# Epsilon of the layer norms added on GpSimd, one copy of turned rows moved to VectorE, and a new table of slots

## The chip, the cores and the metric

The kernel runs on one core of a Trainium2 chip. Its time is the device time of one execution in microseconds (us), and the number compared is the median of several executions. Five engines work beside each other, each through its own list of instructions, in order: TensorE (PE: matrix products and transposes), VectorE (DVE), ScalarE (ACT: exponentials and other functions), GpSimd (POOL) and SyncE (SP, which here starts nearly all the DMAs). They wait for one another only through semaphores.

## The reference

The input x holds 8 sequences of 512 tokens with 128 features. A normalised copy of it goes through 6 layers of attention (16 heads of 8 features) and a feed-forward part; the result is added to x, normalised, goes through a gated network, and is added again. All in fp32.

```python
def layer(h, p):
    q = (h @ wq.T + bq_).reshape(bh, sl, H, DH)
    k = (h @ wk.T + bk_).reshape(bh, sl, H, DH)
    scores = jnp.einsum('blhd,bmhd->bhlm', q, k) * inv_sqrt_d
    w_avg = jax.nn.softmax(scores, axis=-1).mean(axis=1)
    new_w = jax.nn.softmax(CSCALE * w_avg + rel[None], axis=-1)
    sa = jnp.einsum('blm,bme->ble', new_w, h)
    h1 = _ln(h + sa, l1w, l1b)      # (x - mean) * rsqrt(var + 1e-5) * w + b
    h2 = _ln(h1, l2w, l2b)
    ff = jax.nn.relu(h2 @ w1.T + b1_) @ w2.T + b2_
    return (_ln(h2 + ff, l3w, l3b), None)

x = x + layers(_layernorm(x))
x = x + gated_network(_layernorm(x))   # silu(x w1) * (x w2), gelu(. h1), gelu(. h2), . w3
```

## The kernel before

One layer of one sequence is a *unit*: 6 layers by 8 sequences make 48 units, numbered t, the layers outside and the sequences inside. A unit has 64 score tiles of 128 rows by 512 columns: 16 groups (4 blocks of tokens by 4 groups of heads) of 4 tiles. Tile s goes through three engines:

- TensorE makes the scores (line 1015, `sc<-kb,qb`) in one of NS = 5 banks of PSUM. It has to wait until ScalarE has read tile s - 5.
- VectorE takes the negated maximum of each row (line 706, `negmax<-sc`).
- ScalarE takes the exponential with that maximum as bias and sums the rows (line 883, `ex<-sc,negmax`). The exponentials stand in a ring of 20 tiles, which TensorE frees by `sum_heads` (line 1033), so exponential s waits for the group of tile s - 20.

The rest of a unit is laid between the tiles. VectorE inverts the sums (712) and GpSimd makes weights from them (525); TensorE averages the heads with them (1033); ScalarE takes exponentials of the mean (889); TensorE turns them (1041), VectorE multiplies by the fixed relative weights (717, `pt<-m,g_sb`), TensorE attends (1022, `m<-hc,pt`), and VectorE adds the residual (724, `res<-hc,m`). Its last column, E, carries the row's sum, by which the rows are still unscaled; so the first norm needs `zz` = EPS/4 * sum * sum in the place of epsilon (791).

A norm is, on VectorE, 4 `bn_stats` (667), then `spread`: 4 `bn_aggr` (658, `mv<-bn`), which give mean and variance, and the addition of epsilon (662, or 664 with `zz`), which gives `veps`. GpSimd then takes veps to the power -0.5 (`power`, 497, `rstd<-veps,nhalf`), subtracts the mean (`center`, 539), multiplies by `rstd` (`scale`, 533), and by the weight and bias rows (543). Norm 0 is the one after attention (`res`), norm 1 the second (`h`), norm 2 the one after the feed-forward part (`xh`), and norm 3 is used for the input at the start and for the 8 outputs of the last layer. After norm 2, TensorE turns the rows into a bank of PSUM (971, called `norm3_turn` in the table), ScalarE copies them out (938, `h3t<-m`, called `norm3_out`), and TensorE multiplies them by the query and key weights of the next layer (`project`, 1022), VectorE taking the queries out (679) and ScalarE the keys (860). This copy exists for the 40 units whose layer is not the last.

What sets the order is a table written out by hand, `STEP`. All engines walk over slots (g, j): g is the unit whose scores are made, j the tile from 0 to 63. A step with the number n is done for unit t in slot 64 t + n, behind the score work of that slot. So n = 95 stands at tile 31 while the next unit's scores are made. `due` (line 124) looks it up. The number only sets where the instruction stands in the list of its engine; when it runs is a matter of the semaphores. Within one slot the order is that of the loop body. The steps `head_...` belong to the gated network at the end, laid between the last unit's steps behind the last score tile.

Of the kernel before, what the change touches and what calls it, by code (L numbers as in the profile page):

```python
# [5 lines left out]
D, B, S, E, H, F = 6, 8, 512, 128, 16, 512  # L6
# [69 lines left out]
    "project": (194, 199),
    "queries": (195,),
    "keys": (197,),
    "split_q": (223, 223, 226, 233),
    "split_k": (207, 207, 218, 230),  # L80
# [4 lines left out]
    "last_spread": (198,),
    "last_power": (202,),
    "last_apply": (203,),
    "last_turn": (205,),
# [1 line left out]
    "first_stats": (0, 0, 0, 2),  # L90
    "first_spread": (8,),
    "first_power": (15,),
    "first_apply": (12, 42),
    "first_turn": (47,),
    "first_out": (46,),
# [68 lines left out]
def build(nc, x, wqk, bqk, w1t, w2t, cols, rows, fw1, fw2, fh1, fh2, fw3, fcols, frow, gmat, sel, ident, out):  # L164
# [3 lines left out]
    with ctx:  # L168
# [188 lines left out]
        def _(sp):  # L357
# [886 lines left out]
```

## Time and profile before

| | us |
|---|---|
| median of 3 runs (2704.07 to 2704.79) | 2704.5 |
| the profiled execution, own time | 2701.24 |
| its span, from first to last instruction | 2699.4 |
| TensorE busy (share of span) | 2533.7 (94%) |
| VectorE busy | 2452.7 (91%) |
| ScalarE busy | 2437.3 (90%) |
| GpSimd busy | 1432.4 (53%) |

The profile is one execution taken by the hardware profiler; its numbers are microseconds unless marked ns. Busy time is the time in which at least one instruction of the engine ran; two neighbours on an engine overlap a little, so the spacing of two starts says more of what an instruction costs than its duration does. A row of a timeline gives the start, the duration, engine and line, the operation with its output and input, and how many equal ones were merged (x7); square brackets tell the idle time before it and who ended it. The mean granted clock of TensorE was 0.994. First and last exponential of a score tile start at 33.3 and 2388.1 us; the stretch from there to the end is the gated network.

### The profile page before, as it was taken

To read this page: it belongs to the slowest core of one execution; us is meant where nothing else is said; L and a number is where in the kernel's file an instruction comes from. 1 tells how busy PE (TensorE), PEld (TensorE's weight loads), DVE (VectorE), ACT (ScalarE), POOL (GpSimd) and SP (SyncE) were. 2 spreads that over 40 slices of the span, in tenths; PEclk is the share of its full clock that TensorE was granted. 3 is DMA by queue.
4 is the path that set the end of the run, shared out by engine and by line. 5 is a ranking of instruction groups with operands and counts; after the bars stand their busy time and mean duration, and the time that the engine had idled before them with its cause. 6 is when DMAs were issued, how large, how long until landed. Compare 5 with 4: busy or idle time off the path is not lost.

```text
span 2699.4 us, 88896 instructions
## 1 busy us (share of the span) xinstructions
PE 2533.7 (94%) x35336; PEld 1213.7 (45%) x35336; DVE 2452.7 (91%) x5616; ACT 2437.3 (90%) x6799; POOL 1432.4 (53%) x1564
## 2 busy tenths in 40 slices
PE   6899999999999999999999999999999999988999
PEld 1344444444444444444444444444444443446777
DVE  6999999999999999999999999999999999963333
ACT  5999999999999999999999999999999999972222
POOL 3567765565555655655656556555566555544000
PEclk8999999999999999999999999999999999999999
DMA  4222212211122112121121122111211211100000
GB/s 130 66 67 72 81 60 65 68 53 56 54 69 64 48 50 68 53 72 54 53 64 46 52 84 69 55 55 53 64 60 53 69 44 55 50 14 17 16 16 24
DMA packets 98913, 152.86 MB, mean 57 GB/s; under 512 B 17857, under 2 KB 81089, under 8 KB 88897
## 3 DMA queue, kind: packets, MB, share of 16 engines
q1 hardware_dynamic: 97936, 146.26, 17.4%
q8 instruction: 278, 4.55, 0.7%
q14 instruction: 139, 1.13, 0.1%
q10 hardware_dynamic: 560, 0.92, 0.1%
HBM read 92.58 MB, written 41.94 MB: 50 GB/s over the span
## 4 chain that ended last, share of the span: by engine, by line
ACT 35%; DVE 35%; PE 19%; issue 9%; POOL 0%; SPq 0%; DMA 0%; POOLq 0%; ACTq 0%; DVEq 0%
ACT ex L883 31%; DVE negmax L706 25%; PE m L1022 4%; PE mean L1110 3%; PE sc L1110 3%; PE mean L1033 3%; DVE pt L717 2%; PE sc L1015 2%; DVE bn L667 2%; ACT ew L889 2%; ACT relu L934 1%; DVE mv L658 1%; DVE veps L662 1%; PE m L1041 1%; PE m L1122 1%
## 5 line engine op out<-in xcount | busy, mean ns | idle before, releaser
L883 ACT ACTIVATE ex<-sc,negmax 128x512 f32<-128x512 f32 x3072 | 2131.2, 824 | 21.7 <-DVE negmax L706 19.9
L706 DVE TENSOR_REDUCE negmax<-sc 128x1 f32<-128x512 f32 x3072 | 1926.2, 676 | 37.3 <-PE sc L1015 22.8
L1015 PE MATMUL sc<-kb,qb 96*32 96x512 bf16 x12288 | 1060.4, 385 | 107.1 <-ACT ex L883 91.1
L883 ACT ACTIVATION_READ_ACCUMULATOR ex<-sc,negmax 128x1 f32 x3072 | 1058.6, 345 | 0.0
L1033 PE MATMUL mean<-ex,rw 128*32 128x512 f32 x6144 | 803.3, 593 | 7.5 <-ACT ew L889 7.5
L1015 PEld LDWEIGHTS sc<-kb,qb 96*32 96x32 bf16 x12288 | 331.6, 94 | 978.8 <-ACT ex L883 826.9
L525 POOL TENSOR_TENSOR rw<-sel_sb,zinv 128x256 f32<-128x256 f32 x384 | 236.0, 615 | 616.8 <-DVE zinv L712 616.7
L1033 PEld LDWEIGHTS mean<-ex,rw 128*32 128x32 f32 x6144 | 199.4, 110 | 157.0 <-issue 80.0
L1022 PE MATMUL m<-hc,pt 128*32 128x129 f32 x6144 | 205.9, 274 | 6.7 <-DVE pt L717 3.5
L1022 PE MATMUL m<-h2t,w_sb 128*32 128x512 f32 x1536 | 204.8, 597 | 5.4 <-ACT relu L934 2.7
L497 POOL TENSOR_TENSOR rstd<-veps,nhalf 128x4 f32<-128x4 f32 x160 | 163.0, 1019 | 78.1 <-DVE veps L664 54.7
L1022 PE MATMUL m<-w_sb,relu 128*32 128x128 f32 x6144 | 200.3, 272 | 0.8 <-ACT relu L934 0.8
L1022 PEld LDWEIGHTS m<-hc,pt 128*32 128x32 f32 x6144 | 170.8, 110 | 48.6 <-DVE pt L717 28.4
L543 POOL TENSOR_TENSOR h<-h,row 128x512 f32<-128x512 f32 x144 | 184.6, 1282 | 7.8 <-POOL h L533 0.4
L1022 PEld LDWEIGHTS m<-w_sb,relu 128*32 128x32 f32 x6144 | 170.5, 109 | 35.8 <-ACT relu L934 23.6
L934 ACT ACTIVATE relu<-m,col 128x512 f32<-128x512 f32 x192 | 163.2, 850 | 12.3 <-PE m L1022 12.3
L539 POOL TENSOR_TENSOR xh<-xh,mv 128x512 f32<-128x512 f32 x48 | 50.1, 1044 | 194.7 <-DVE veps L662 194.7
L889 ACT ACTIVATE ew<-mean 128x512 f32<-128x512 f32 x192 | 133.8, 697 | 0.8 <-PE mean L1033 0.8
L1041 PE MATMUL m<-id_sb,ew 128*128 128x128 f32 x768 | 125.6, 286 | 8.3 <-DVE res L724 0.6
L717 DVE TENSOR_TENSOR pt<-m,g_sb 128x512 f32<-128x512 f32 x192 | 130.1, 678 | 0.0
L1041 PEld LDWEIGHTS m<-id_sb,ew 128*128 128x128 f32 x768 | 80.5, 140 | 75.6 <-issue 39.1
L543 POOL TENSOR_TENSOR h<-h,rb 128x512 f32<-128x512 f32 x48 | 61.6, 1284 | 87.9 <-PE m L971 87.9
(111 smaller groups left out, 2450.1 us busy)
## 6 DMA issues: line engine op xcount, KB each, us to landing
kb<-qk_split SPq DMA_DIRECT2D x288, 128.0 KB
qb<-qk_split SPq DMA_DIRECT2D x568, 64.0 KB
qk_split<-kp SPq DMA_DIRECT2D x144, 128.0 KB, 1.8
qk_split<-qp SPq DMA_DIRECT2D x141, 128.0 KB, 1.8
hc<-hs SPq DMA_DIRECT2D x48, 256.0 KB, 2.7
xin<-x SPq DMA_DIRECT2D x16, 256.0 KB, 2.7
fh_raw<-fh SPq DMA_DIRECT2D x2, 1024.0 KB, 5.2
y_kept<-xin SPq DMA_DIRECT2D x8, 256.0 KB, 2.0
```

The lines of the kernel that those rows point to most:

```text
L497: nc.gpsimd.tensor_tensor(rstd[:, k, :], veps[:, k, :], nhalf[:, :], ALU.pow).then_inc(rstd_ready[k], 1)
L525: nc.gpsimd.tensor_tensor(rw[:, c:c + ZB, :], sel_sb[:, :].rearrange("p (a q) -> p a q", a=1).to_broadcast([P, ZB, QS]), zinv[:, c:c + ZB] ...
L543: nc.gpsimd.tensor_tensor(dst, src[:, :, :], r.to_broadcast([P, NT, E]), op).then_inc(done, 1)
L706: nc.vector.tensor_reduce(negmax[:, s % RT:s % RT + 1], sc[s % NS][:, :], AX, ALU.max, negate=True) \
L717: nc.vector.tensor_tensor(pt[:, i % 2, :, :], m0[:, :].rearrange("p (c l) -> p c l", c=NT), g_sb[:, i, :, :], ALU.mult).then_inc(pt_ready, 1)
L883: nc.scalar.activation(ex[:, s % ET, :], sc[s % NS][:, :], ACT.Exp, bias=negmax[:, c:c + 1], accum_out=zsum[:, c:c + 1]).then_inc(exp_read ...
L889: nc.scalar.activation(ew[:, i % 2, :], mean[:, :], ACT.Exp).then_inc(ew_ready, 1)
L934: nc.scalar.activation(relu[:, c, :], m1[:, :], ACT.Relu, bias=col[RUN[t] % 2][:, C_B1 + c:C_B1 + c + 1]).then_inc(relu_ready, 1)
L1015: ins = nc.tensor.matmul(sc[s % NS][h * QS:h * QS + QS, :], qb[t % 2][:, h % 2, g, h // 2, r:r + QS], kb[t % 2][:, g, h // 2, :], start=Tr ...
L1022: ins = nc.tensor.matmul(dst[n * QS:n * QS + QS], lhsT[:, n * QS:n * QS + QS], rhs, start=start, stop=stop)
L1033: ins = nc.tensor.matmul(mean[n * QS:(n + 1) * QS, :], rw[:, s % RT, :], ex[:, s % ET, :], start=(g == 0), stop=(g == NG - 1))
L1041: ins = nc.tensor.transpose(m0[:, c * P:c * P + P], ew[:, i % 2, c * P:c * P + P], id_sb[:, :])
```

## The change

There are four parts.

1. `spread` on VectorE ends behind the 4 `bn_aggr`. The addition of epsilon, and for norm 0 the two factors of `zz` (before one instruction on VectorE, now two, through a new tile `ze`), stand on GpSimd in `power`, ahead of the power itself: one more small instruction (128 x 4 elements) for norms 1, 2 and 3, and three for norm 0.
2. The subtraction of the mean (`center`) waits for `mv_ready` instead of `veps_ready`. VectorE waits for the earlier `veps` and `zz` before it writes over `mv` and `res`.
3. The copy `h3t<-m` of the 40 units goes from ScalarE to VectorE.
4. Most numbers of `STEP` are new. Two more small memsets stand at the start, and the waits on `filled` count to 7.

```diff
-    "stats0": (66, 76, 77, 83),
-    "spread": (83, 95, 175),
-    "power": (80, 106, 176),
-    "apply0": (82, 85),
+    "stats0": (75, 76, 78, 83),
+    "spread": (83, 94, 175),
+    "power": (84, 110, 178),
+    "apply0": (85, 86),
...
-    "norm3_out": (189,),
+    "norm3_out": (191,),
...
             def power(k, n):
+                if k == 0:
+                    gp.wait_ge(res_ready, n * NT)
+                    nc.gpsimd.tensor_tensor(ze[:, :], res[:, :, E], eps4[:, :], ALU.mult).then_inc(ze_ready, 1)
+                    gp.wait_ge(ze_ready, n)
+                    nc.gpsimd.tensor_tensor(zz[:, :], ze[:, :], res[:, :, E], ALU.mult).then_inc(zz_ready, 1)
+                    gp.wait_ge(zz_ready, n)
+                gp.wait_ge(mv_ready[k], n)
+                nc.gpsimd.tensor_tensor(veps[:, k, :], mv[:, k, :, 1], (eps if k else zz)[:, :], ALU.add).then_inc(veps_ready[k], 1)
                 gp.wait_ge(veps_ready[k], n)
                 nc.gpsimd.tensor_tensor(rstd[:, k, :], veps[:, k, :], nhalf[:, :], ALU.pow).then_inc(rstd_ready[k], 1)
...
             def center(dst, src, k, t):
-                gp.wait_ge(veps_ready[k], t + 1)
+                gp.wait_ge(mv_ready[k], t + 1)
...
-            def spread(k, n, plus):
+            def spread(k, n):
                 dve.wait_ge(bn_ready[k], n * NT)
+                wait_later(dve, veps_ready[k], n - 1)
                 for i in range(NT):
                     ins = nc.vector.bn_aggr(mv[:, k, i, :], bn[:, k, i, :])
                 ins.then_inc(mv_ready[k], 1)
-                dve.wait_ge(mv_ready[k], n)
-                if plus is None:
-                    nc.vector.tensor_scalar(veps[:, k, :], mv[:, k, :, 1], EPS, None, ALU.add).then_inc(veps_ready[k], 1)
-                else:
-                    nc.vector.tensor_tensor(veps[:, k, :], mv[:, k, :, 1], plus, ALU.add).then_inc(veps_ready[k], 1)
...
                 if i == 0:
                     wait_later(dve, centered[0], t)
+                    wait_later(dve, zz_ready, t)
...
                 for t in due("spread", 0, g, j):
-                    nc.vector.scalar_tensor_tensor(zz[:, :], res[:, :, E], EPS / 4, res[:, :, E], ALU.mult, ALU.mult) \
-                        .then_inc(zz_ready, 1)
-                    dve.wait_ge(zz_ready, t + 1)
-                    spread(0, t + 1, zz[:, :])
+                    spread(0, t + 1)
...
+                for t in due("norm3_out", 0, g, j):
+                    dve.wait_ge(xh3t_ready, late_input(t) + 1)
+                    nc.vector.tensor_copy(h3t[:, :], m1[:, :]).then_inc(ht_ready, 1)
...
-                for t in due("norm3_out", 0, g, j):
-                    act.wait_ge(xh3t_ready, late_input(t) + 1)
-                    nc.scalar.activation(h3t[:, :], m1[:, :], ACT.Copy).then_inc(ht_ready, 1)
```

Of the table's other numbers these matter here: the queries' read (`queries`) goes from 195 to 197 and the second product of `project` from 199 to 200; `sum_heads` for group 7 goes from 47 to 50.

First, VectorE in the middle of a unit, from the last statistics of norm 0 (`bn<-res`) to the end of norm 1 (`bn<-h`), before:

```order
L667 BN_STATS bn<-res 128x6
L791 SCALAR_TENSOR_TENSOR zz<-res 128x4
L658 BN_AGGR mv<-bn 128x2 x4
L664 TENSOR_TENSOR veps<-mv,zz 128x4
L706 TENSOR_REDUCE negmax<-sc 128x1 x7
L712 RECIPROCAL zinv<-zsum 128x8
L706 TENSOR_REDUCE negmax<-sc 128x1 x4
L667 BN_STATS bn<-h 128x6 x4
L706 TENSOR_REDUCE negmax<-sc 128x1
L658 BN_AGGR mv<-bn 128x2 x4
L662 TENSOR_SCALAR veps<-mv 128x4
```

and with the change:

```order
L732 SCALAR_TENSOR_TENSOR res<-hc,m 128x129
L674 BN_STATS bn<-res 128x6
L670 BN_AGGR mv<-bn 128x2 x4
L713 TENSOR_REDUCE negmax<-sc 128x1 x10
L719 RECIPROCAL zinv<-zsum 128x8
L713 TENSOR_REDUCE negmax<-sc 128x1
L674 BN_STATS bn<-h 128x6 x4
L670 BN_AGGR mv<-bn 128x2 x4
L713 TENSOR_REDUCE negmax<-sc 128x1 x5
```

The factor `zz` and both additions `veps` are gone; the last residual now stands directly ahead of the last statistics of norm 0, and the statistics of norm 1 directly ahead of their `bn_aggr`, with no score tile between them.

Second, GpSimd at norm 0 in the middle of a unit (`rstd` is the power, `h<-res,mv` subtracts the mean, `h<-h,row` are weight and bias, the casts belong to the splitting of queries and keys), before:

```order
L525 TENSOR_TENSOR rw<-sel_sb,zinv 128x256
L497 TENSOR_TENSOR rstd<-veps,nhalf 128x4
L539 TENSOR_TENSOR h<-res,mv 128x512
L533 TENSOR_TENSOR h<-h,rstd 128x512
L543 TENSOR_TENSOR h<-h,row 128x512
L330 CAST kp<-kf 128x512
L543 TENSOR_TENSOR h<-h,row 128x512
L525 TENSOR_TENSOR rw<-sel_sb,zinv 128x256
L326 CAST qp<-qf 128x512
```

and with the change:

```order
L501 TENSOR_TENSOR ze<-res,eps 128x4
L503 TENSOR_TENSOR zz<-ze,res 128x4
L506 TENSOR_TENSOR veps<-mv,zz 128x4
L508 TENSOR_TENSOR rstd<-veps,nhalf 128x4
L550 TENSOR_TENSOR h<-res,mv 128x512
L327 CAST qp<-qf 128x512
L544 TENSOR_TENSOR h<-h,rstd 128x512
L554 TENSOR_TENSOR h<-h,row 128x512 x2
L536 TENSOR_TENSOR rw<-sel_sb,zinv 128x256
L329 TENSOR_TENSOR kf<-kf,kp 128x512
```

Three small instructions now stand ahead of the power. One cast of 512 columns stands between power and bias before and after, at another place.

Third, the turn of the unit, where the rows for the next layer's projection are copied out (`h3t<-m`). Before it is ScalarE's:

```order
L883 ACTIVATE ex,zsum<-sc,negmax 128x512 x17
L889 ACTIVATE ew<-mean 128x512
L883 ACTIVATE ex,zsum<-sc,negmax 128x512 x14
L938 ACTIVATE h3t<-m 128x512
L883 ACTIVATE ex,zsum<-sc,negmax 128x512 x2
L889 ACTIVATE ew<-mean 128x512
L883 ACTIVATE ex,zsum<-sc,negmax 128x512 x6
L860 ACTIVATE kf<-m,bqk_sb 128x512
```

and with the change it is VectorE's, between the last residual's region and the queries' read (`qf<-m`):

```order
L713 TENSOR_REDUCE negmax<-sc 128x1 x6
L719 RECIPROCAL zinv<-zsum 128x8
L732 SCALAR_TENSOR_TENSOR res<-hc,m 128x129
L713 TENSOR_REDUCE negmax<-sc 128x1 x2
L823 COPY h3t<-m 128x512
L713 TENSOR_REDUCE negmax<-sc 128x1 x3
L719 RECIPROCAL zinv<-zsum 128x8
L713 TENSOR_REDUCE negmax<-sc 128x1 x3
L686 TENSOR_SCALAR qf<-m,bqk_sb 128x512
```

VectorE has one more instruction of 512 columns there, six score tiles ahead of the queries' read.

## Rows read from the trace of the kernel before

**Rows 1.** Busy time by engine in three stretches; x is the number of instructions.

```profile
1000.00:1491.00 491.00, 466.31 (x7124) 212.17 (x7118) 483.37 (x1101) 487.87 (x1391) 283.39 (x311) 1.00 0.19 58
2050.00:2343.00 293.00, 275.75 (x4196) 122.58 (x4192) 289.92 (x699) 292.46 (x834) 163.80 (x174) 1.00 0.18 55
2390.00:2699.00 309.00, 290.50 (x1595) 210.37 (x1594) 119.20 (x237) 91.25 (x123) 39.91 (x35) 0.99 0.05 17
```

**Rows 2.** Groups of instructions by line: VectorE, from 1000 to 1491 us.

```profile
L706 DVE TENSOR_REDUCE negmax<-sc 128x1 f32<-128x512 f32 x641 | 401.8, 675 | 6.2 <-PE sc L1015 2.9
```

**Rows 3.** Groups by line: VectorE, the whole run.

```profile
L730 DVE CAST hid_hi<-fh_raw 128x512 fp32r<-128x512 f32 x32 | 13.9, 435 | 20.8 <-PE mean L1110 20.3
```

**Rows 4.** Timeline of VectorE: start us, duration us, engine, line, operation, count.

```profile
1127.08 0.28 DVE L667 BATCH_NORM_STATS2 bn<-res 128x6 f32<-128x128 f32 x1
1127.28 0.15 DVE L791 SCALAR_TENSOR_TENSOR zz<-res 128x4 f32<-128x4 f32 x1
1127.47 0.38 DVE L658 BATCH_NORM_AGGREGATE mv<-bn 128x2 f32<-128x6 f32 x4
1127.88 0.16 DVE L664 TENSOR_TENSOR veps<-mv,zz 128x4 f32<-128x4 f32 x1
1127.96 4.27 DVE L706 TENSOR_REDUCE negmax<-sc 128x1 f32<-128x512 f32 x7
...
1135.02 0.86 DVE L667 BATCH_NORM_STATS2 bn<-h 128x6 f32<-128x128 f32 x4
...
1136.58 0.37 DVE L658 BATCH_NORM_AGGREGATE mv<-bn 128x2 f32<-128x6 f32 x4
1136.98 0.57 DVE L662 TENSOR_SCALAR veps<-mv 128x4 f32<-128x4 f32 x1
1137.46 2.47 DVE L706 TENSOR_REDUCE negmax<-sc 128x1 f32<-128x512 f32 x4
1139.86 0.67 DVE L717 TENSOR_TENSOR pt<-m,g_sb 128x512 f32<-128x512 f32 x1
1140.46 1.27 DVE L706 TENSOR_REDUCE negmax<-sc 128x1 f32<-128x512 f32 x2
...
1149.40 0.37 DVE L658 BATCH_NORM_AGGREGATE mv<-bn 128x2 f32<-128x6 f32 x4
1149.80 0.17 DVE L662 TENSOR_SCALAR veps<-mv 128x4 f32<-128x4 f32 x1
1149.87 3.07 DVE L706 TENSOR_REDUCE negmax<-sc 128x1 f32<-128x512 f32 x5
```

**Rows 5.** Timeline of ScalarE, from 1110 to 1113 us.

```profile
1110.84 0.66 ACT L938 ACTIVATE h3t<-m 128x512 f32<-128x512 f32 x1
1111.32 0.76 ACT L883 ACTIVATE ex<-sc,negmax 128x512 f32<-128x512 f32 x1
...
1111.98 0.77 ACT L883 ACTIVATE ex<-sc,negmax 128x512 f32<-128x512 f32 x1
```

**Rows 6.** Timeline of ScalarE, from 1018 to 1020 us.

```profile
1018.88 0.82 ACT L860 ACTIVATE kf<-m,bqk_sb 128x512 f32<-128x512 f32 x1
1019.45 0.83 ACT L883 ACTIVATE ex<-sc,negmax 128x512 f32<-128x512 f32 x1
```

**Rows 7.** Timeline of GpSimd, from 1110 to 1160 us.

```profile
1128.13 1.02 POOL L497 TENSOR_TENSOR rstd<-veps,nhalf 128x4 f32<-128x4 f32 x1 [1.11 <-DVE veps L664]
1129.12 1.04 POOL L539 TENSOR_TENSOR h<-res,mv 128x512 f32<-128x512 f32 x1
...
1133.21 1.28 POOL L543 TENSOR_TENSOR h<-h,row 128x512 f32<-128x512 f32 x1
...
1136.92 0.61 POOL L330 CAST qp<-qf 128x512 bf16<-128x512 f32 x1
```

**Rows 8.** Groups by line: GpSimd, the whole run.

```profile
L581 POOL TENSOR_TENSOR rb<-row 128x128 f32<-128x128 f32 x6 | 2.7, 455 | 0.0
```

**Rows 9.** Groups by line: ScalarE, the whole run.

```profile
L905 ACT ACT_TABLE_LOAD x6 | 7.7, 1283 | 0.1
```

More of the change, by code:

```diff
@@ L45 @@
 STEP = {
-    "invert_sums": (12, 18, 26, 37, 42, 52, 58, 66),
-    "row_weights": (14, 16, 28, 42, 45, 50, 67, 73),
-    "sum_heads": (21, 22, 25, 26, 32, 34, 45, 47, 52, 57, 61, 64, 69, 72, 73, 75),
+    "invert_sums": (12, 17, 29, 36, 42, 51, 61, 66),
+    "row_weights": (9, 19, 29, 44, 44, 51, 67, 69),
+    "sum_heads": (21, 21, 25, 27, 32, 34, 45, 50, 52, 56, 61, 64, 69, 71, 74, 75),
     "exp_mean": (25, 47, 63, 73),
     "transpose_mean": (30, 53, 68, 79),
-    "relative": (35, 56, 73, 78),
@@ L52 @@
-    "attend": (40, 59, 76, 82),
-    "residual": (40, 61, 76, 82),
-    "stats0": (66, 76, 77, 83),
-    "spread": (83, 95, 175),
-    "power": (80, 106, 176),
-    "apply0": (82, 85),
-    "norm1_weight": (90,),
-    "norm1_bias": (91,),
+    "relative": (35, 55, 74, 78),
+    "attend": (40, 59, 76, 81),
+    "residual": (40, 61, 76, 83),
+    "stats0": (75, 76, 78, 83),
+    "spread": (83, 94, 175),
+    "power": (84, 110, 178),
+    "apply0": (85, 86),
+    "norm1_weight": (88,),
+    "norm1_bias": (88,),
@@ L60 @@
     "stats1": (94, 94, 94, 94),
-    "apply1": (107, 107),
+    "apply1": (107, 110),
     "norm2_turn": (143,),
     "norm2_out": (142,),
-    "token_weight": (141,),
+    "token_weight": (136,),
     "token_bias": (143,),
     "up": (146, 151, 156, 158),
-    "relu": (146, 150, 153, 158),
+    "relu": (146, 150, 153, 157),
     "down": (163, 165, 170, 172),
     "add": (172,),
-    "stats2": (173, 174, 174, 174),
-    "apply2": (175, 176),
+    "stats2": (173, 173, 174, 174),
+    "apply2": (175, 178),
@@ L72 @@
     "norm3_turn": (191,),
-    "norm3_out": (189,),
-    "norm3_weight": (178,),
+    "norm3_out": (191,),
+    "norm3_weight": (180,),
     "norm3_bias": (182,),
[L76 to L80, printed above, removed]
+    "project": (195, 200),
+    "queries": (197,),
+    "keys": (200,),
+    "split_q": (213, 223, 233, 233),
+    "split_k": (211, 222, 222, 229),
     "last_weight": (185,),
-    "last_bias": (192,),
@@ L83 @@
-    "last_add": (193,),
+    "last_bias": (194,),
+    "last_add": (194,),
     "last_stats": (193,),
[L85 to L88, printed above, removed]
+    "last_spread": (195,),
+    "last_power": (198,),
+    "last_apply": (198,),
+    "last_turn": (203,),
     "last_keep": (203,),
[L90 to L95, printed above, removed]
@@ L108 @@
-    "head_gelu": (69, 82, 85, 87, 92, 94, 99, 110, 111, 117, 118, 134, 153, 156, 170, 173),
-    "head_split": (94, 100, 114, 115, 118, 145, 145, 148),
+    "first_stats": (0, 0, 0, 1),
+    "first_spread": (6,),
+    "first_power": (6,),
+    "first_apply": (12, 14),
+    "first_turn": (48,),
+    "first_out": (45,),
+    "first_token": (44,),
+    "first_project": (50, 55),
+    "first_queries": (52,),
+    "first_keys": (55,),
+    "first_split_q": (55, 61, 61, 61),
+    "first_split_k": (55, 62, 64, 68),
@@ new lines @@
+    "head_high": (0, 3, 18, 25, 30, 32, 38, 53),
+    "head_low": (9, 17, 31, 39, 47, 64, 64, 67),
+    "head_first": (66, 66, 70, 70, 73, 76, 78, 79),
+    "head_silu": (64, 65, 65, 67, 67, 73, 84, 92),
+    "head_gate": (63, 69, 71, 71, 74, 76, 78, 85),
+    "head_square": (75, 83, 87, 93, 94, 97, 110, 112, 112, 125, 127, 135, 141, 157, 179, 192),
+    "head_gelu": (79, 88, 92, 93, 97, 103, 110, 120, 120, 122, 135, 135, 161, 169, 172, 177),
+    "head_split": (88, 93, 98, 110, 128, 132, 144, 169),
@@ L200, in build @@
         rstd = sb("rstd", [P, 4, NT])
-        nhalf = sb("nhalf", [P, NT])
+        nhalf, eps, eps4 = sb("nhalf", [P, NT]), sb("eps", [P, NT]), sb("eps4", [P, NT])
+        ze = sb("ze", [P, NT])
         h1 = sb("h1", [P, NT, E])
@@ L283, in build @@
         sa_ready = sem("sa_ready")
-        zz_ready = sem("zz_ready")
+        ze_ready, zz_ready = sem("ze_ready"), sem("zz_ready")
         res_ready = sem("res_ready")
@@ L423, in _ @@
                 sp.dma_start(qk_dram[0, 3 + n, :, :], kp[n][:, :]).then_inc(kept, 16)
-            sp.wait_ge(filled, 5)
+            sp.wait_ge(filled, 7)
             sp.wait_ge(q_kept, 48)
@@ L686, in _ @@
                 wait_later(dve, first_ready, b)
-                spread(3, b + 1, None)
+                spread(3, b + 1)
                 dve.wait_ge(rstd_ready[3], b + 1)
@@ L800, in _ @@
                     wait_later(dve, centered[1], t)
-                    spread(1, t + 1, None)
+                    spread(1, t + 1)
                 for t in due("add", 0, g, j):
@@ L824, in _ @@
                     wait_later(dve, centered[3], b - PRE)
-                    spread(3, b + 1, None)
+                    spread(3, b + 1)
                 for b in due("first_queries", 0, g, j):
@@ L834, in _ @@
                 for t in due("last_spread", 0, g, j):
-                    spread(3, B + OUTER[t] + 1, None)
+                    spread(3, B + OUTER[t] + 1)
                 for n in range(2 * CH):
@@ L871, in _ @@
             first_copy(1)
-            act.wait_ge(filled, 5)
+            act.wait_ge(filled, 7)
             act.wait_ge(q_kept, 48)
```

19 lines of the change are left out of this document (5 added, 14 removed).

## The prediction

> **What bounds the kernel now.** I read the busy shares first: TensorE, VectorE and ScalarE all stand at 90% or more, GpSimd at 53%, so the end is set by three engines that pass tiles round, and the table of stretches has to say which. From 1000 to 1491 us VectorE is busy 483.37 of 491.00 us and ScalarE 487.87 [rows 1]; 641 score maxima fall into it [rows 2], which is 10.0 units of 64, so a unit takes 49.1 us. VectorE has 7.6 us idle in ten units, 0.76 per unit. ScalarE's busy time overstates its load: two exponentials in a row start 0.66 us apart (1111.32 and 1111.98) although each is shown with over 0.7 us [rows 5]. Counted by starts ScalarE needs 64 x 0.66 + 5 x 0.48 (four exponentials of the mean and the copy, the copy being 1110.84 to 1111.32 [rows 5]) + 6 x 0.57 (h2t, four relu and the keys; the keys' row is 1018.88 to 1019.45 [rows 6]; that the others are like it is my reading of their kind and size) = 42.2 + 2.4 + 3.4 = 48.1 us, 1.0 below the period. VectorE by its idle time needs 49.1 - 0.76 = 48.3. So VectorE is the fullest engine, ScalarE 0.2 behind it, and 0.7 us per unit is lost because only five banks lie between them: where one has a bunch of extra work, the other runs dry. In the last layer (2050 to 2343) VectorE's idle time is 3.1 us in 293, and TensorE alone carries the stretch behind the last exponential, 290.5 of 309 us [rows 1].
>
> **Part 1, epsilon on GpSimd.** Timeline of VectorE, one unit [rows 4].
> Norm 0: from the last statistics (1127.08) to the next maximum (1127.96) 0.88 us. What stays is statistics of 0.28, a hand-over of 0.03 (the `bn_aggr` that end at 1127.85 are followed by the dependent addition at 1127.88), and the four `bn_aggr`, 0.37, of which the last 0.08 overlap with an independent follower, as the four maxima's 2.47 end 0.07 behind the next start (1137.46, 1139.86). That is 0.28 + 0.03 + 0.29 = 0.60. The last residual now stands right ahead of these statistics and has to finish first; that costs about the same 0.07 + 0.03 = 0.10. Saved: 0.18.
> Norm 1: from `bn_aggr` (1136.58) to the next maximum (1137.46) 0.88, now 0.29; but the statistics stand right ahead now, which costs 0.11. Saved: 0.48.
> Norm 2: 1149.40 to 1149.87, 0.47, now 0.29. Saved: 0.18.
> Together 0.84 us per unit. Norm 1's addition is the dearest: it is shown with 0.57 us against 0.17 for the same instruction in norm 2. It ended at 1137.55, within 0.02 of the GpSimd cast that began at 1136.92 with 0.61 [rows 7]: it stood waiting for that cast. The Trainium skill (SBUF — State Buffer, "Who interferes with whom") says that a VectorE instruction in a 2-port mode, which an SBUF-to-SBUF tensor_scalar can be, is locked out for the whole of a GpSimd instruction that began first; by that rule the trace agrees (0.57 against 0.17). The skill (Perfetto Trace Analysis, "Optimizing Scalar/DVE Operations") also warns that moving work from VectorE to GpSimd may not help because they share that port. That would cost something only where VectorE keeps instructions that use the shared port; the two kinds that the trace shows doing so go away, so I price it at nothing.
> Norms of units 0 to 46 end under score tiles: 47 x 0.84 = 39.5 us. The extra spreads of norm 3 save 0.18 each: 7 outputs and 6 inputs, 2.3 us.
>
> On GpSimd the new instructions are not in the trace. The nearest rows: 128 columns with 0.455 us [rows 8] and 512 columns with 1.28 [rows 7], which put 4 columns at 0.455 - 124 x 0.825/384 = 0.19 us; and from above the power itself on the same 4 columns, 1.02 us [rows 7]. I take 0.19 plus 0.08 between dependent ones, since a power is another computation than a sum. Five of them are 1.4 us per unit on an engine with 20 us free (283.39 busy of 491 [rows 1]). What counts is norm 0's chain. Before, the power began at 1128.13, the bias ended at 1133.21 + 1.28 = 1134.49 [rows 7], and VectorE came for it at 1135.02 [rows 4]: 0.53 us to spare. Counted from the last statistics' start, `mv` is now ready after 0.28 + 0.03 + 0.37 = 0.68 instead of 0.77 us; `ze` and `zz` run beside it; the addition and the power follow, so the power starts after about 0.68 + 0.05 + 0.27 = 1.00 us, against 1128.13 - 1127.08 = 1.05 before. VectorE itself comes 0.28 earlier. So 0.3 us stay to spare and nothing is paid.
>
> **Part 2, the copy on VectorE.** 40 copies of 512 fp32 columns out of PSUM. The trace has none on VectorE. Nearest from PSUM: the product `pt`, 1139.86 to 1140.46, 0.60 us [rows 4]; the maxima are as long. From below, a cast of 512 columns within SBUF, 0.435 us shown [rows 3], some 0.36 by starts. I take 0.60, the row with the same source. The Trainium skill (VectorE: DVE Perf Modes, "Why PSUM operands drop a tier") says that an fp32 operand in PSUM leaves only the 1x mode; by it the upper row holds, by the SBUF cast the copies would be 9.6 us cheaper in all. No run here shows yet which. 40 x 0.60 = 24.0 us more on VectorE. ScalarE is relieved of 40 x 0.48 = 19.2 us, which buys nothing directly, since it isn't the fullest. The copy waits for the turn in the same slot; TensorE issues that behind the score tile whose maximum VectorE takes first (0.60), longer than the four transposes, so I price this wait at nothing. Behind it on VectorE are queued the next maxima; if the turn is late, they are.
>
> **Part 3, the slots.** VectorE now needs 48.3 - 0.84 + 0.60 = 48.1 us per inner unit, ScalarE 47.6. Whether the 0.76 us of idle time shrinks hangs on the bunches. Two of VectorE's are thinner (the statistics of norms 0 and 1 with their additions), and at the unit's turn the loads of both come nearer to each other. Against it, `sum_heads` of group 7 goes from slot 47 to 50, two slots behind the exponential that needs its place, and the second projection is now three slots behind the queries' read instead of four. I take 0.1 us less idle per unit, 40 x 0.1 = 4 us; the ends are 0.76 less and 0.45 more.
> At the start GpSimd's addition stands ahead of two powers on the way to the first tile: +0.3 us. In the tail ScalarE switches its function tables once more than before, 1.28 us [rows 9]; TensorE's list is the same but for two or three exchanged places: I count +1.3.
>
> **Sum.** -39.5 - 2.3 + 24.0 - 4.0 + 0.3 + 1.3 = -20.2 us on the profiled execution, 2701.24 to 2681.0. The median of the runs shown is 3.3 above that execution; so the forecast is 2704.5 - 20 = 2684 us (-0.75%).
>
> **Rivals.**
> A, the waits go too. VectorE waits for TensorE at the turn of the unit (2.9 us of its idle time there is behind score tiles [rows 2]); if the copy falls into such gaps and the thinner bunches halve the idle time, 40 x 0.38 = 15 us go instead of 4: 2673 us. For it speaks that ScalarE's load drops by 0.5 us per unit as well; against it, that VectorE remains the fullest.
> B, the slots eat it. A late turn, the queries' read that TensorE's second projection waits for, or group 7's `sum_heads` costs 0.45 us more idle time per unit, 18 us over 40 units, where I counted 4 less: 2684 + 22 = 2706, and half of it 2695. For it: TensorE is busy 466 of 491 us [rows 1] and packed at the unit's turn.
> C, slower, by one mechanism: a small GpSimd instruction costs like the power, 1.0 us, not 0.19. `ze`, `zz` and the addition then end 3 x 1.08 = 3.2 us behind the last residual instead of 1.0, the power starts 2.2 us late, and with 0.3 us to spare VectorE stands still 1.9 us ahead of norm 1's statistics in each of 47 units: +89 us, 2704.5 - 20 + 89 = 2773. It decides from about 0.35 us each, where 3 x (0.35 + 0.08) is the 1.3 us that the spare time allows. For it speaks only that the power's row has the same shape; against it the line through 128 and 512 columns.
> That the change doesn't do what it says (VectorE's list as long as before) is excluded by the order of its instructions.
>
> **How the numbers follow.** Forecast 0.62 (its own range 2677 to 2692), A 0.15, B 0.15, C 0.08. A change of under 0.2%, 5.4 us, is what a measurement of this kernel can't tell from none. Below 2699.1 lie the forecast, A, and a third of B: 0.82. Within 0.2% half of B and a little of C's mild forms: 0.09. Slower: the rest of B and of C: 0.09. The range goes from 2669 (A) to 2702 (B in part).
>
> **What would show it.** Right: no `zz` and `veps` on VectorE, a copy with starts 0.60 apart, a unit of 48.5 to 48.7 us, VectorE's idle time 0.6 to 0.7 per unit; small GpSimd additions of about 0.2 us; no idle time ahead of `bn<-h`; the stretch behind the last exponential within 2 us of 311. Wrong: additions near 1 us and VectorE waiting ahead of `bn<-h` (C); a period of 49 us with waits for the turn, or exponentials waiting for `sum_heads` (B); a period under 48.4 (A). If ScalarE turned out as the fullest, 0.48 and not VectorE's 0.24 us would be what a unit gains, and the first step would be wrong.

## The result

| | before | with the change |
|---|---|---|
| median, us | 2704.35 | 2676.53 (2675.93 to 2677.58) |
| ratio | | 0.9898 (0.9885 to 0.9910) |
| span of the profiled execution, us | 2699.4 | 2674.7 |
| first exponential of a score tile starts at | 33.3 | 33.5 |
| last one starts at | 2388.1 | 2364.5 |
| from there to the end of the span | 311.3 | 310.2 |

The change is 1.0% faster, 28 us by the medians; 20 were forecast. The two profiled executions lie 24.7 us apart, because the one before ran 3 us below its median. Nearly all of that lies under the score tiles: the stretch from the first to the last exponential is 23.8 us shorter, the start 0.2 longer, the tail 1.1 shorter. By the starts of the exponentials, a unit of the four middle layers takes 48.45 us instead of 49.11 (21.3 us in 32 units); the first and the last layer give 1.3 and 1.2 us, each over its 8 units.

The same three stretches of the changed kernel (the stretch and its length, then PE, PEld, DVE, ACT and POOL busy, granted clock, DMA share, GB/s); they answer to [rows 1], and the first two windows again hold ten and six units:

```profile
1000.00:1485.00 485.00, 465.32 (x7148) 204.90 (x7140) 478.32 (x1072) 484.17 (x1382) 293.72 (x362) 1.00 0.20 59
2030.00:2322.00 292.00, 273.94 (x4198) 119.83 (x4191) 286.94 (x674) 291.54 (x835) 176.01 (x213) 1.00 0.18 55
2368.00:2674.00 306.00, 288.77 (x1594) 209.40 (x1592) 119.14 (x239) 92.66 (x124) 41.67 (x43) 0.99 0.05 17
```

VectorE is idle for 6.7 us in ten units, where it was 7.6. The norms of one unit on VectorE, which answer to [rows 4]:

```profile
1116.60 0.34 DVE L732 SCALAR_TENSOR_TENSOR res<-hc,m 128x129 f32<-128x129 f32 x1
1116.98 0.29 DVE L674 BATCH_NORM_STATS2 bn<-res 128x6 f32<-128x128 f32 x1
1117.31 0.38 DVE L670 BATCH_NORM_AGGREGATE mv<-bn 128x2 f32<-128x6 f32 x4
1117.60 5.44 DVE L713 TENSOR_REDUCE negmax<-sc 128x1 f32<-128x512 f32 x9
...
1124.60 0.86 DVE L674 BATCH_NORM_STATS2 bn<-h 128x6 f32<-128x128 f32 x4
1125.55 0.38 DVE L670 BATCH_NORM_AGGREGATE mv<-bn 128x2 f32<-128x6 f32 x4
1125.85 2.45 DVE L713 TENSOR_REDUCE negmax<-sc 128x1 f32<-128x512 f32 x4
...
1138.64 0.37 DVE L670 BATCH_NORM_AGGREGATE mv<-bn 128x2 f32<-128x6 f32 x4
1138.92 2.45 DVE L713 TENSOR_REDUCE negmax<-sc 128x1 f32<-128x512 f32 x4
...
1149.46 0.68 DVE L823 COPY h3t<-m 128x512 f32<-128x512 f32 x1
1150.06 1.88 DVE L713 TENSOR_REDUCE negmax<-sc 128x1 f32<-128x512 f32 x3
```

`zz` and `veps` are gone. From the last statistics of norm 0 (1116.98) to the next maximum 0.62 us; `bn_aggr` to maximum 0.30 and 0.28 in norms 1 and 2; the copy out of PSUM takes 0.60 by starts. So the forecast's upper row was the right one. The wait of norm 1's addition behind a GpSimd cast [rows 4, 7] has no place any more. On GpSimd, norm 0 now reads (answers to [rows 7]):

```profile
1117.03 0.20 POOL L501 TENSOR_TENSOR ze<-res,eps 128x4 f32<-128x4 f32 x1 [0.37 <-DVE res L732]
1117.30 0.21 POOL L503 TENSOR_TENSOR zz<-ze,res 128x4 f32<-128x4 f32 x1
1117.83 0.20 POOL L506 TENSOR_TENSOR veps<-mv,zz 128x4 f32<-128x4 f32 x1 [0.32 <-DVE mv L670]
1118.11 1.02 POOL L508 TENSOR_TENSOR rstd<-veps,nhalf 128x4 f32<-128x4 f32 x1
...
1121.84 2.63 POOL L554 TENSOR_TENSOR h<-h,row 128x512 f32<-128x512 f32 x2
```

and the new addition over the whole run:

```profile
L506 POOL TENSOR_TENSOR veps<-mv,eps 128x4 f32<-128x4 f32 x112 | 23.0, 205 | 24.7 <-DVE mv L670 24.6
```

A small addition takes 0.2 us, the power behind it 1.02 as before. The two instructions merged in the last row of the timeline are norm 0's weight and bias; they end at 1124.47, and VectorE comes for them at 1124.60 without waiting (it starts 0.08 us before the shown end of its previous instruction).

### The profile page after: what moved, and what is told of

It is laid out like the page before. It is cut to its first block and busy times, and to the rows that moved or that the text cites. A ratio compares the mean times of both kernels' runs of the same rounds, so it can differ in the third digit from the quotient of the medians.

```text
span 2674.7 us, 89003 instructions
## 1 busy us (share of the span) xinstructions
PE 2523.1 (94%) x35336; PEld 1185.6 (44%) x35336; DVE 2423.9 (91%) x5448; ACT 2421.3 (91%) x6760; POOL 1486.5 (56%) x1822
## 5 line engine op out<-in xcount | busy, mean ns | idle before, releaser
L891 ACT ACTIVATE ex<-sc,negmax 128x512 f32<-128x512 f32 x3072 | 2096.2, 767 | 14.9 <-DVE negmax L713 10.5
L1020 PE MATMUL sc<-kb,qb 96*32 96x512 bf16 x12288 | 1048.6, 385 | 92.4 <-ACT ex L891 72.3
L891 ACT ACTIVATION_READ_ACCUMULATOR ex<-sc,negmax 128x1 f32 x3072 | 883.8, 288 | 0.0
L1038 PE MATMUL mean<-ex,rw 128*32 128x512 f32 x6144 | 790.0, 594 | 7.6 <-ACT ew L897 7.6
L1020 PEld LDWEIGHTS sc<-kb,qb 96*32 96x32 bf16 x12288 | 321.4, 94 | 996.7 <-ACT ex L891 862.6
L1038 PEld LDWEIGHTS mean<-ex,rw 128*32 128x32 f32 x6144 | 189.1, 110 | 147.4 <-issue 69.8
L942 ACT ACTIVATE relu<-m,col 128x512 f32<-128x512 f32 x192 | 144.5, 753 | 10.3 <-PE m L1027 10.3
L897 ACT ACTIVATE ew<-mean 128x512 f32<-128x512 f32 x192 | 124.5, 648 | 0.0
L544 POOL TENSOR_TENSOR h<-h,rstd 128x512 f32<-128x512 f32 x96 | 99.7, 1039 | 7.5
```

The costliest lines, as they stand in the source:

```text
L891: nc.scalar.activation(ex[:, s % ET, :], sc[s % NS][:, :], ACT.Exp, bias=negmax[:, c:c + 1], accum_out=zsum[:, c:c + 1]).then_inc(exp_read ...
L897: nc.scalar.activation(ew[:, i % 2, :], mean[:, :], ACT.Exp).then_inc(ew_ready, 1)
L942: nc.scalar.activation(relu[:, c, :], m1[:, :], ACT.Relu, bias=col[RUN[t] % 2][:, C_B1 + c:C_B1 + c + 1]).then_inc(relu_ready, 1)
L1020: ins = nc.tensor.matmul(sc[s % NS][h * QS:h * QS + QS, :], qb[t % 2][:, h % 2, g, h // 2, r:r + QS], kb[t % 2][:, g, h // 2, :], start=Tr ...
L1038: ins = nc.tensor.matmul(mean[n * QS:(n + 1) * QS, :], rw[:, s % RT, :], ex[:, s % ET, :], start=(g == 0), stop=(g == NG - 1))
```

## Where the limit stands

Two neighbouring tiles of ScalarE show what sets the unit. Before, at the end of VectorE's stretch (norm 2 at slots 44 to 47):

```profile
1148.40 0.70 ACT L883 ACTIVATE ex<-sc,negmax 128x512 f32<-128x512 f32 x1
...
1149.51 0.69 ACT L883 ACTIVATE ex<-sc,negmax 128x512 f32<-128x512 f32 x1 [0.31 <-DVE negmax L706]
```

With the change, at the same place:

```profile
1137.88 0.70 ACT L891 ACTIVATE ex<-sc,negmax 128x512 f32<-128x512 f32 x1
...
1138.76 0.69 ACT L891 ACTIVATE ex<-sc,negmax 128x512 f32<-128x512 f32 x1
```

Two starts that follow each other without a wait are 0.66 us apart. Here they are 1.11 and 0.88 apart: 0.45 us of waiting before, 0.21 after. The bracket tells only what lies beyond the shown end of the last instruction (0.31), and after the change there is none at all, though ScalarE waited. So I went through ScalarE's starts over ten units of each kernel, took 0.66 us off each exponential, 0.48 off the mean's exponentials and the copy, and 0.57 off the others, and what was over 0.03 us I counted as waiting, by the tile behind which it stands ("46: 0.45" is 0.45 us per unit between the exponentials of tiles 46 and 47). The rest of the period is ScalarE's own load.

| kernel | unit, us | load of ScalarE | waits of ScalarE | at tiles |
|---|---|---|---|---|
| before | 49.12 | 48.2 | 0.88 | 19: 0.13, 43: 0.30, 46: 0.45 |
| the change | 48.46 | 47.75 | 0.71 | 5: 0.14, 19: 0.19, 43: 0.16, 46: 0.21 |
| e1 | 50.17 | 48.3 | 1.92 | 3: 0.86, 9: 0.13, 19: 0.44, 43: 0.16, 46: 0.22, 55: 0.08 |
| e2 | 48.88 | 48.2 | 0.67 | 25: 0.07, 43: 0.39, 46: 0.21 |
| e3 | 49.15 | 47.8 | 1.37 | 3: 0.60, 43: 0.28, 46: 0.43 |
| e4 | 48.74 | 47.8 | 0.94 | 3: 0.44, 43: 0.29, 46: 0.21 |
| e5 | 49.83 | 48.2 | 1.59 | 3: 0.93, 9: 0.13, 19: 0.15, 43: 0.16, 46: 0.22 |
| e6 | 49.02 | 47.8 | 1.25 | 5: 0.26, 19: 0.50, 43: 0.16, 46: 0.22, 55: 0.08 |
| e7 | 49.04 | 47.8 | 1.27 | 5: 0.26, 19: 0.18, 43: 0.16, 46: 0.22, 63: 0.39 |
| e8 | 48.98 | 48.3 | 0.66 | 5: 0.14, 19: 0.11, 43: 0.19, 46: 0.21 |
| e9 | 48.93 | 48.3 | 0.64 | 19: 0.23, 43: 0.20, 46: 0.21 |
| e10 | 48.46 | 47.8 | 0.64 | 5: 0.12, 19: 0.17, 43: 0.15, 46: 0.21 |
| e11 | 49.05 | 47.8 | 1.26 | 5: 0.12, 19: 0.16, 43: 0.15, 44: 0.18, 45: 0.32, 46: 0.32 |
| e12 | 48.97 | 48.3 | 0.64 | 19: 0.24, 43: 0.20, 46: 0.21 |

In the kernel before and in the change ScalarE waits at three or four places and runs without a gap everywhere else. The change takes 0.49 us off its load (the copy) and 0.17 off its waits.

For whom it waits isn't the same at each place. Behind tiles 19 and 46, and with the copy on VectorE behind 3, 5 and 63, the next exponential starts 0.03 us after the end of its maximum: it waited for VectorE. Behind tile 43 it did not. There the maximum had been ready for 0.75 to 1 us in every kernel of the table but e11 (0.39), and the exponential starts 0.14 us after the end of TensorE's `sum_heads`, which frees its place in the ring. Before:

```profile
1145.89 1.03 PE L1033 MATMUL mean<-ex,rw 128*32 128x512 f32 x8
1146.11 0.99 ACT L883 ACTIVATE ex<-sc,negmax 128x512 f32<-128x512 f32 x1
1147.07 0.70 ACT L883 ACTIVATE ex<-sc,negmax 128x512 f32<-128x512 f32 x1
```

So 0.15 to 0.39 us per unit of waiting is TensorE's, not VectorE's; no run moved that step by itself. The wait behind tile 3 in e1 and e5 is of this kind too.

## The experiments

Three parts (epsilon on GpSimd, the copy on VectorE, the table) make eight combinations. Medians in us, each less the median of the kernel before in the same session (2702.8 to 2705.0); the 95% intervals of the ratios reach 0.0009 to 0.0014 to either side, 2.5 to 4 us.

| | copy on ScalarE | copy on VectorE |
|---|---|---|
| old table, epsilon on VectorE | 0 | +1.8 (e3) |
| old table, epsilon on GpSimd | -12.3 (e2) | -18.3 (e4) |
| new table, epsilon on VectorE | +42.2 (e1) | +0.7 (e6) |
| new table, epsilon on GpSimd | +24.3 (e5); copy at slot 189: -11.4 (e9) | -27.8 (the change) |

The texts put on record ahead of the runs speak of theories. Theory 1 is the prediction's: the fullest engine, VectorE, sets the unit. Theory 2 is its rival, given anew for each run. Theory 3 is that a step came too late in its list. Theory 4 is that the limit goes from engine to engine within a unit, and only the load of the one whose stretch it is counts.

**e1**, the kernel before with the whole new table.

```diff
-    "spread": (83, 95, 175),
-    "power": (80, 106, 176),
+    "spread": (83, 94, 175),
+    "power": (84, 110, 178),
...
-    "norm3_out": (189,),
+    "norm3_out": (191,),
...
-    "queries": (195,),
+    "queries": (197,),
```

> The kernel before with the new table of slots and nothing else: epsilon stays on VectorE, the copy h3t stays on ScalarE. Theory 1 (the fullest engine sets the unit, the table moves only the waits a little, as predicted): 4 us less than before, 2700 us, period of a unit 49.0 us. Theory 2 (most of the 28 us come from the table, which evens out bunches and removes waits that hide inside the spacing of the score maxima): at least 15 us less, 2689 us or below, period 48.7.

2746.9 us, ratio 1.0155 (1.0141 to 1.0169). Both theories missed: the table alone makes the kernel slower. From 1000 to 1490 us TensorE waits 10 times, 13.3 us in all, for the copy `h3t`. e5 has the same fault, and e9 its cause.

**e2**, epsilon on GpSimd as in the change (parts 1 and 2 of it, which no run took apart), the old table, the copy on ScalarE. Against the change, beside the table:

```diff
-                for t in due("norm3_out", 0, g, j):
-                    dve.wait_ge(xh3t_ready, late_input(t) + 1)
-                    nc.vector.tensor_copy(h3t[:, :], m1[:, :]).then_inc(ht_ready, 1)
+                for t in due("norm3_out", 0, g, j):
+                    act.wait_ge(xh3t_ready, late_input(t) + 1)
+                    nc.scalar.activation(h3t[:, :], m1[:, :], ACT.Copy).then_inc(ht_ready, 1)
```

> Epsilon's additions on GpSimd, the old table, the copy h3t still on ScalarE. Theory 1: VectorE's load falls by 0.84 us per unit to 47.5, ScalarE with 48.1 becomes the fullest, so a unit falls by 0.5 to 0.7 us and the kernel by 25 to 33 us, 2672 to 2680 us. Theory 2: the waits of the old table stay, 8 to 12 us less, about 2694 us.

2692.4 us, 0.9955 (0.9942 to 0.9967): -12.3, near theory 2's number. VectorE's instructions other than the maxima take 0.96 us less per unit, counted from start to start in the trace, where 0.84 was forecast. The unit is only 0.24 shorter: the other 0.73 turn up behind VectorE's score maxima as waiting, most of it too short to be shown as idle time (9.2 us in 485, before 7.6).

**e3**, the copy on VectorE at slot 191, the rest as before.

```diff
-    "norm3_out": (189,),
+    "norm3_out": (191,),
...
+                    nc.vector.tensor_copy(h3t[:, :], m1[:, :]).then_inc(ht_ready, 1)
...
-                    nc.scalar.activation(h3t[:, :], m1[:, :], ACT.Copy).then_inc(ht_ready, 1)
```

> The copy h3t on VectorE (its slot 191, where the turn stands, else the old table), epsilon still on VectorE. Theory 1: VectorE is the fullest and gets 0.60 us more in 40 units, +24 us, 2728 us. Theory 2: VectorE waits at this place anyway and ScalarE is relieved; +5 to +10 us at most, 2712 us.

2706.5 us, 1.0008 (0.9999 to 1.0017). Not +24: ScalarE's load falls by 0.4 to 0.5 us per unit, and its waits rise by 0.49, with a new one of 0.60 behind tile 3.

**e4**, the change with the old table (the copy at 191).

```diff
-    "power": (84, 110, 178),
+    "power": (80, 106, 176),
...
-    "queries": (197,),
+    "queries": (195,),
```

> Epsilon on GpSimd and the copy on VectorE, with the old table (only the copy's slot is 191). It is the change without its slots. Theory 1: -40 + 24 = -16 us, 2688 us. Theory 2: the loads alone bring little, -5 us, 2699 us. The difference to the change's 2676.5 is what the table is worth once the loads are moved.

2686.4 us, 0.9932 (0.9919 to 0.9946): -18.3. Theory 1's number, but not for its reason, since its two terms (-40 and +24) are wrong by themselves. ScalarE in this kernel, at tile 3, behind the copy and the queries' read on VectorE (slots 191 and 195):

```profile
1010.90 0.82 ACT L891 ACTIVATE ex<-sc,negmax 128x512 f32<-128x512 f32 x1
...
1012.01 0.69 ACT L891 ACTIVATE ex<-sc,negmax 128x512 f32<-128x512 f32 x1 [0.19 <-DVE negmax L713]
```

1.11 us instead of 0.66. In the change, with the queries' read at 197, there is no wait at tile 3 and 0.14 at tile 5. The table is worth 9.5 us (e4 to the change), and this is where the unit shows most of it: waits at tile 3 or 5 from 0.44 to 0.14, at 43 from 0.29 to 0.16, at 19 from nothing to 0.19. That it is the queries' number which did it is read from the place of the wait; it wasn't moved by itself.

**e5**, the change with the copy on ScalarE, at the table's slot 191 (diff as in e2).

> The change with the copy h3t left on ScalarE (its slot 191): what the move of the copy is worth inside the change. Theory 1 (VectorE is the fullest): VectorE gets 24 us lighter, ScalarE at 48.1 per unit becomes the limit; 2666 to 2672 us, 5 to 10 us faster than the change. Theory 2 (with epsilon gone VectorE and ScalarE are level, and a unit is limited by ScalarE's load plus its waits): 5 to 15 us slower than the change, 2682 to 2692 us.

2727.1 us, 1.0089 (1.0076 to 1.0103): 52 above the change, far beyond both. TensorE's waits from 1000 to 1485 us (us in total, times, the longest):

```profile
PE m L1027 <- ACT h3t L943: 13.3, 10, 1.3
```

Ten times 1.3 us, once per unit, the query projection at slot 195 waits for the copy. `sum_heads` stands behind it in TensorE's list and is late by it, and ScalarE in turn waits for that, 0.93 us per unit behind tile 3. Of this the profile shows what lies beyond the shown ends:

```profile
ACT ex L888 <- PE mean L1038: 6.7, 10, 0.7
```

**e9**, e5 with one number back.

```diff
-    "norm3_out": (191,),
+    "norm3_out": (189,),
```

> The kernel of run e5 (change with the copy h3t left on ScalarE) with the copy at slot 189 instead of 191. In e5 TensorE's query projection waited 1.3 us for this copy in every unit. Theory 3 (lateness: at 191 ScalarE's list, which runs some four tiles behind TensorE's, reaches the copy after TensorE wants it at 195): the wait goes and the kernel falls by 40 us or more, to 2680 to 2688 us, 3 to 11 us above the change, which is then what moving the copy off ScalarE is worth. Rival (ScalarE's load is the cause): it stays above 2715 us.

2693.5 us, 0.9960 (0.9947 to 0.9972). The 36 us were the lateness. The lists run apart: when TensorE starts this projection in e9, it has begun the scores of tile 3 and ScalarE is at the exponential of tile 63 of the unit before, four tiles behind. So slot 191 (tile 63) on ScalarE comes no earlier than slot 195 (tile 3) on TensorE. It stays 16.4 above the change, more than the 3 to 11 expected: that is the worth of the copy's move with the new table, 0.41 us in each of 40 units, close to the 0.48 that ScalarE is relieved of. ScalarE is then shown busy for the whole stretch (its waits are hidden by the shown durations) and VectorE is idle for 13.3 us in ten units:

```profile
1000.00:1485.00 485.00, 461.75 (x7080) 208.76 (x7084) 471.73 (x1048) 484.39 (x1380) 291.06 (x360) 1.00 0.20 59
```

**e6**, the new table and the copy on VectorE, epsilon on VectorE as before: e1 with the copy moved.

```diff
+                    nc.vector.tensor_copy(h3t[:, :], m1[:, :]).then_inc(ht_ready, 1)
...
-                    nc.scalar.activation(h3t[:, :], m1[:, :], ACT.Copy).then_inc(ht_ready, 1)
```

> The new table and the copy on VectorE, epsilon still on VectorE. Theory 1: +24 - 4, 2724 us, VectorE's idle time per unit under 0.7. Theory 2: the table makes up for the copy, 2700 to 2710 us. Against the change's 2676.5 it gives what epsilon on GpSimd is worth with everything else in place: 0.84 x 47 = 40 us by the prediction.

2703.4 us, 1.0001 (0.9992 to 1.0010). Against it the change is 28.5 us faster: epsilon's worth with everything else in place, where VectorE is loaded with the copy. With the copy on ScalarE and the old table it was 12.3. ScalarE's load is the same in e6 and the change; the waits differ, behind tile 19, where norm 0's `spread` stands, 0.50 against 0.19 us, and behind 5, 0.26 against 0.14.

**e7**, the change with a second copy on VectorE.

```diff
+                    wait_later(dve, spared, t)
+                    nc.vector.tensor_copy(spare[:, :], m1[:, :]).then_inc(spared, 1)
                     nc.vector.tensor_copy(h3t[:, :], m1[:, :]).then_inc(ht_ready, 1)
```

> The change with one more VectorE copy of the same 512 columns out of the same bank in each of 40 units, into a spare bf16 tile, 0.60 us by starts. It measures how much of VectorE's load reaches the unit. Theory 1: VectorE is the fullest, all of it, +24 us, 2700 us. Rival: VectorE has 0.7 us of idle time per unit that takes it in, under +8 us.

2698.6 us, 0.9985 (0.9976 to 0.9993): 22 to 24 above the change. The second copy stands ahead of the needed one, which it delays too: TensorE now waits 0.4 us for that one in each unit, and 0.05 us of it reach ScalarE, behind tile 3. The rest is VectorE's load itself: ScalarE gets a new wait of 0.39 us behind tile 63, for the maximum, and 0.12 more behind 5. At this place VectorE's load counts in full.

**e8**, the change with a second read of the keys' bank on ScalarE.

```diff
+                    act.wait_ge(k_ready, late_input(t) + 1)
+                    wait_later(act, spared, t)
+                    nc.scalar.activation(spare[:, :], m1[:, :], ACT.Identity,
+                                         bias=bqk_sb[LAYER_OF[late_input(t)] % 2][:, 1:2]).then_inc(spared, 1)
                     keys(late_input(t))
```

> The change with one more ScalarE activation of 512 columns out of the keys' bank in each of 40 units, into a spare bf16 tile, 0.57 us by starts. Theory 1: ScalarE has about 0.8 us to spare in a unit of 48.4 (its load is 47.6), so under +8 us, 2684 us at most. Rival: the change left ScalarE as the limit with its waits, +23 us, 2699 us.

2696.8 us, 0.9979 (0.9970 to 0.9987): 20 to 22 above the change for 23 us of work. Its waits stay as they were (0.66 against 0.71 us per unit), so the work goes on top. Theory 1 fell here: ScalarE had nothing to spare.

**e10, e11 and e12**, the change with one more instruction of 512 columns at another slot in 40 units, on VectorE at 24 (e10, shown) and 40 (e11), on ScalarE at 52 (e12).

```diff
+    "extra": (24,),
...
+                for t in due("extra", 0, g, j):
+                    wait_later(dve, spared, t)
+                    nc.vector.tensor_reduce(spare[:, :], g_sb[:, 0, :, :].rearrange("p c l -> p (c l)"), AX, ALU.max, negate=True) \
+                        .then_inc(spared, 1)
```

and for e12, in ScalarE's list:

```diff
+                for t in due("extra", 0, g, j):
+                    wait_later(act, spared, t)
+                    nc.scalar.activation(spare[:, :], g_sb[:, 0, :, :].rearrange("p c l -> p (c l)"), ACT.Copy).then_inc(spared, 1)
```

> The change with one more VectorE maximum of 512 columns (0.60 us, from SBUF into a spare column) at slot 24 in 40 units, where ScalarE has its relus and VectorE shows its waits for score tiles. Theory 4 (the limit goes from engine to engine within a unit, and only the one whose stretch it is counts): VectorE is not it here, at most +8 us, 2677 to 2685 us. Rival (VectorE as full as e7 said, anywhere in the unit): +20 to +24 us, 2697 to 2700.

> The same instruction at slot 40, in VectorE's own stretch (residual, the feed-forward addition and norm 2 lie at 40 to 47). Theory 4: nearly all of 0.60 x 40 us, +18 to +24 us, 2695 to 2700 us. Rival (the load counts as a sum over the unit): the same as at slot 24, within 3 us.

> The change with one more ScalarE copy of 512 columns (from SBUF into a spare bf16 tile, about 0.5 us) at slot 52 in 40 units, where ScalarE has nothing but exponentials from 48 to 62. Theory 4: ScalarE is not the limit here, at most +8 us, 2677 to 2685 us. Rival (ScalarE's load counts wherever it stands, as at the keys in e8): +17 to +20 us, 2694 to 2697.

e10: 2679.1 us, 0.9907 (0.9893 to 0.9920), 2 above the change, which lies within the intervals. e11: 2700.0 us, 0.9981 (0.9973 to 0.9990), 23 above it. e12: 2694.8 us, 0.9966 (0.9954 to 0.9978), 18 above it. For VectorE theory 4 holds: the same 0.60 us is free at slot 24 and paid in full at 40. The extra one of e10 and what follows it:

```profile
1027.39 0.68 DVE L812 TENSOR_REDUCE spare<-g_sb 128x1 f32<-128x512 f32 x1
1027.98 3.08 DVE L716 TENSOR_REDUCE negmax<-sc 128x1 f32<-128x512 f32 x5
```

Ten units of e10 and of e11, as stretches:

```profile
1000.00:1485.00 485.00, 465.39 (x7128) 205.34 (x7126) 483.14 (x1082) 484.33 (x1383) 294.12 (x362) 1.00 0.19 59
```

```profile
1000.00:1485.00 485.00, 459.72 (x6988) 201.03 (x6976) 478.33 (x1071) 480.58 (x1366) 290.41 (x358) 1.00 0.19 57
```

In e10 VectorE is busy for 483.1 of 485 us and the unit is no longer for it; in e11 it has 6.7 us idle, as in the change, and the unit is 0.6 us longer: ScalarE waits for VectorE's maxima behind tiles 44, 45 and 46, by 0.6 us more. The extra instruction of e12 takes 0.52 us by starts, 21 us in all. For ScalarE theory 4 failed: at slot 52, where it has nothing but exponentials, its extra work counts nearly as at slot 8.

## Why the prediction was right, and where it wasn't

The direction and the range held, and so did the prices of the instructions. That the sum came within 8 us was luck in good part: it was put together from two large terms that were both wrong and leaned against each other.

- *Prices on VectorE.* Norms 0, 1, 2 were to need 0.60, 0.29, 0.29 us; they need 0.62, 0.30, 0.28. The copy 0.60, as taken from `pt` [rows 4].
- *Small instructions on GpSimd*, 0.19 us by a line through two wider ones [rows 7, 8]: 0.205. Rival C is out. Norm 0's chain was to keep 0.3 us to spare; it keeps 0.13. The power starts 1.13 us after the last statistics' start (1116.98 to 1118.11) where 1.00 was forecast, mainly because the addition starts 0.14 after `mv` is ready and not 0.05. The prediction also speaks of two kinds of VectorE instructions that waited for GpSimd; its rows show one, norm 1's addition, a wait that stands behind no semaphore.
- *The start* +0.2 (forecast +0.3), *the tail* -1.1 (forecast +1.3); I had priced the additional table switch as if ScalarE were the limit there, which TensorE is [rows 1]. Why it came out shorter was not tried.
- *The step that failed* is "VectorE is the fullest engine, ScalarE 0.2 behind it", and with it "ScalarE is relieved of 40 x 0.48 = 19.2 us, which buys nothing directly, since it isn't the fullest". I compared two loads that lay 0.2 us apart and let the smaller count for nothing. ScalarE runs without gaps but for the few waits above, and its load counts at each of the places tried (e8 20 to 22, e12 18 us for 23 and 21 us of work). VectorE's load counts where its bunches make ScalarE wait: at the unit's turn (e7) and from 40 to 47 (e11), not at 24 (e10). The prediction had named the sign, 0.48 us per unit if ScalarE were the fullest; the unit gained 0.66, of which 0.49 are ScalarE's load and 0.17 its waits. The last layer says the same without a run of its own: it has no copy in either kernel, VectorE is relieved of the same additions, and a unit falls only from 48.83 to 48.66 us (its slots are new as well).
- *So the terms of the sum.* Epsilon: forecast -41.8, measured -12.3 with the old table and the copy on ScalarE, -20.1 (e3 to e4) or -28.5 (e6 to the change) with the copy on VectorE. In e2 the wait at tile 46 falls from 0.45 to 0.21 us, the one at 43 rises by 0.09, the one at 19 (0.13) goes, and the rest of the relief lies where VectorE wasn't the limit. The copy: forecast +24.0, measured +1.8 with epsilon still on VectorE (e3), -6.0 (e2 to e4) and -16.4 (e9 to the change). It takes 0.48 us off ScalarE and puts 0.60 on VectorE at the unit's turn, where it makes a new wait of 0.44 us with the old table and 0.14 with the new.
- *The slots:* forecast -4, measured -9.5 once both loads had moved, -1.1 with only the copy moved (e3 to e6) and +0.9 with only epsilon moved (e2 to e9), neither of which is clear of the intervals. The table pays for the copy's move, as it seems by setting the queries' read two slots later (e4). Of the feared losses, `sum_heads` of group 7 at slot 50 costs nothing that shows: it frees the place of tile 48, and no wait of ScalarE stands behind tile 47.
- Rival A, 2673 us, is nearer to 2676.5 than the forecast's 2684, though not by its mechanism: VectorE's idle time didn't halve (7.6 us in 491 to 6.7 in 485). Rival B is out.

The profile would have told it beforehand: the shown duration of ScalarE's exponentials grows from tile to tile (0.76 and 0.77 in [rows 5], 0.83 in [rows 6], 0.99 at 1146.11 above) and falls back to 0.69 or 0.70 behind a wait. Before, it grows from tile 47 through the unit's turn to tile 19 of the next unit. I read that as overstated busy time; in these traces it is also the sign of an engine that hasn't waited since.

e10 and e12 together point to a version that wasn't run: one of the relu reads moved from ScalarE to VectorE at about slot 24, where VectorE takes 0.6 us for 2 us in all, while ScalarE's 0.57 us would count, if what held at slots 8 and 52 holds there too: 23 us at most in 40 units, an estimate from those runs.

## What to carry to other kernels

Where two engines pass tiles through a few buffers and their loads lie within a per cent or two, there need not be one limit: price a move at both ends and by its place. Look for where each engine last waited, by the spacing of starts rather than by the idle time shown, and ask of each piece of work whether it stands in a stretch that makes the other wait. And when a step goes to another engine, its number in a common table means another time: the lists run apart, here by up to four tiles with five banks between them (e5 to e9: 36 us for two slots).

## What the hardware showed besides

A GpSimd sum or product of 128 x 4 fp32 elements took 0.20 us on average over 256 cases, a power of the same shape 1.02 us over 160. ScalarE's exponentials with accumulation start 0.66 us apart when nothing holds them, whatever duration is shown, from 0.68 to 1.05 us. A VectorE copy of 512 fp32 columns out of PSUM starts 0.60 us ahead of its follower, as a maximum or a product does; out of the same bank ScalarE needs 0.48.
